# Local attention on Trainium2: the V product in four 64x64 quadrants, with the output projection in column halves

## The chip, the cores and the metric

The kernel runs on one core of one Trainium2 chip. The time is device time in microseconds (us) of one execution. Three runs of the kernel before took 3222.01, 3215.9 and 3220.32 us; the median is 3220.32 us.

## The reference, cut to what matters

The program is four layers of cross attention and feed-forward blocks on 128 sequences of 64 tokens with 128 features, all in fp32. The change touches only the last block, which holds two rounds (DEPTH = 2) of local attention, each followed by a gated MLP. With 64 tokens in a sequence and a window of 64, there is one window, so the attention is causal over the sequence itself:

```python
DIM, HEADS, DIM_HEAD, WINDOW = 128, 8, 64, 64      # INNER = 512
def _layer(x, wqkv, qs, ksc, wo, ...):             # x: 128 sequences x 64 tokens x 128
    h = shift_token(x)                             # half of the features come from the token before
    q, k, v = jnp.split(h @ wqkv, 3, axis=-1)      # each 512 wide: 8 heads of 64
    q = l2norm(q) * qs;  k = l2norm(k) * ksc
    q, k = rotary_xpos(q, k)
    sim = jnp.einsum('bhwid,bhwjd->bhwij', bq, bk) # bq is 8 * q
    attn = jax.nn.softmax(jnp.where(mask, -big, sim), axis=-1)
    out = jnp.einsum('bhwij,bhwjd->bhwid', attn, bv)
    x = x + o @ wo                                 # o: 512 wide, wo: 512x128
    ...                                            # gated MLP
```

## The kernel before, in words

The residual stream `x` stays in SBUF as 64 tiles of 128 tokens (two sequences of 64) by 128 features. `local_attention(l)` goes over these tiles in 16 groups of four (GT = 4). Every engine runs its own written-out order of steps, `body(g)`, once a group, in a hardware loop (`run_tiles`); semaphores tie the engines together, and `wait_tile(engine, signal, g, t)` waits until tile t has passed a step. The work is software pipelined: in the step for tile u, TensorE handles tiles u to u+3.

The order on TensorE for each u (a "tile turn" below) is:

- `scores(u+1)`, L1981 and L1989: a causal mask as four bf16 matmuls, then 16 matmuls of 64x64 stationary by 64 columns. Sequence b goes to the column half b (PSUM partitions 64b and on), the head parity j is the row half (SBUF partitions 64j and on) and the PSUM bank. So four (row half, column half) pairs follow one another.
- `project_qk(u+3)`, L1949 and L1950, and `project_v(u+3)`, L1960: V comes out with the parity of the head as the partition half.
- `weigh_values(u)`, L2014: the product V^T P^T, 16 matmuls of 64x64 by 64 columns into `ps_o`. Row half j writes column half j, for both sequences, so only two of the four pairs occur.
- in the first tile turn of a group, `transpose_window(g+1)`, L1941: four transposes for the next group.
- `turn_qk(u+2)`, L1970: eight 128x128 transposes of the normalised queries and keys.
- `project_o(u)`, L2022: four 128x128x128 matmuls that accumulate in `ps_pj`. It contracts over pairs of heads.
- `turn_probs(u+1)`, L2000: four transposes of the probabilities.

An fp32 matmul is two records in the trace, a transpose or a bf16 matmul is one.

The other engines: ScalarE squares q and k (L2059), takes the exponentials (L2082) and copies PSUM to SBUF (`copy_ot` L2092, `copy_v` L2072, `copy_qk` L2078, `copy_pt` L2087). VectorE does row maxima and the subtraction (L2187, L2190), row sums and the reciprocal (L2198, L2200), the rotary products (L2166 and L2173 twice), the squares' sums (L2178, L2181) and the residual (L2204). GpSimd adds the two rotary products (`unite`, L2130), refines the norms' inverse roots (L2136 to L2140), scales q and k with them (`normalise_qk`, L2143) and scales the probabilities (L2123). In the trace `kblk` is the room of the rotated q and k and of V, `big_flat` that of `qk_t`, `pl`, `pt` and `ot`.

Weights that are needed late are loaded by DMAs that GpSimd issues between its steps in the first cross attention (`late_loads`, issued at L743; 50 of them, five after each of ten groups).

Of the kernel before, what the change touches and what calls it, by code (L numbers as in the profile page):

```python
# [18 lines left out]
F32 = mybir.dt.float32  # L19
ACT = mybir.ActivationFunctionType  # L20
# [3 lines left out]
P = 128  # L24
S = 64
# [23 lines left out]
LHEADS, LD, LPAIRS = 8, 64, 4  # L49
INNER = LHEADS * LD  # L50
HALF = LD // 2
DEPTH = 2
# [35 lines left out]
def build_program(nc, w, x_in, ctx_t, mask_l2, mask_l3, out):  # L88

    with ExitStack() as ctx:  # L90
        def sb(name, shape, dt=F32):
            return ctx.enter_context(nc.sbuf_tensor(name, shape, dt))
# [3 lines left out]
        def signal(name, per=0, ahead=0):  # L96
            if name not in signals:
                assert per == 0 or name in GROUP_SIGNALS, name
                signals[name] = Signal(ctx.enter_context(nc.semaphore(name)))
            signals[name].opens(per, ahead)  # L100
            return signals[name]
# [75 lines left out]
        one_less_mu = {n: sb("one_less_mu_" + n, [P, 1]) for n in "rk"}  # L177
        w_qkv = [sb(f"w_qkv{l}", [P, 3 * INNER]) for l in range(DEPTH)]
        w_lo = [sb(f"w_lo{l}", [P, LPAIRS, P]) for l in range(DEPTH)]

        rot_base = sb("rot_base", [P, 4, LD])
        rot = [sb(f"rot{l}", [P, 4, LD]) for l in range(DEPTH)]
# [21 lines left out]
        ps_s = ctx.enter_context(nc.psum_tensor("ps_s", [P, 4, 512], F32))  # L204
        ps_scores = [ps_s[:, 2 * i:2 * i + 2, :] for i in range(2)]
        ps_pt = ctx.enter_context(nc.psum_tensor("ps_pt", [P, 2, 512], F32))
        ps_o = ctx.enter_context(nc.psum_tensor("ps_o", [P, 512], F32))
        ps_pj = ctx.enter_context(nc.psum_tensor("ps_pj", [P, 512], F32))


        carried = signal("carried", GT)
# [12 lines left out]
        late_loads = [(attn_w[n][:, :], w[n]) for n in attn_w if not n.startswith("L0")]  # L224
# [7 lines left out]
        late_loads += [(mu[n][:, :], w["mu_" + n]) for n in "rk"]  # L232
        late_loads += [(rot_base[:, :, :], w["rot"]), (rot_scale[:, :, :, :], w["rot_scale"])]
        for l in range(DEPTH):
            late_loads += [(w_qkv[l][:, :], w["wqkv"][l]), (w_lo[l][:, :, :], w["lo"][l]),
                           (w_up1[l][:, :], w["up1"][l]),
                           (b_up1[l][:, :], w["b_up1"][l]), (w_dn[l][:, :, :], w["dn"][l]),
                           (b_dn[l][:, :], w["b_dn"][l]), (ln_gb[l][:, :], w["ln"][l])]
# [171 lines left out]
        added = signal("added")  # L410
# [171 lines left out]
        def wait_past(eng, s, g, k):  # L582

            value = s.at(g, k)
            if not isinstance(value, int) or value > s.base:
                eng.wait_ge(s.sem, value)
# [1292 lines left out]
        def local_attention(l):  # L1879
# [25 lines left out]
            ot_copied = signal("ot_ready", GT)  # L1905
            y_ready = signal("y_ready", GT)

            bank_qk, bank_ts = ps_scores
            bank_v, bank_p = ps_pt[:, 0, :], ps_pt[:, 1, :]
            square = probs[0][:, :, :]  # L1910
            nrm, nlog, nroot, nstep = (small[n][:, 0, :] for n in "bcde")

# [6 lines left out]
            def wait_tile(eng, s, g, t, done=None):  # L1919

                each = s.per // GT
                wait_past(eng, s, g, each * t + (each if done is None else done))
# [4 lines left out]
            with nc.Block() as block:  # L1927
                @block.sync
                def _(sp):
                    move_window(sp, 1 if l == 0 else 0)  # L1930

                @block.tensor
                def _(pe):
# [69 lines left out]
                    def weigh_values(g, t):  # L2003
                        wait_tile(pe, pt_copied, g, t)
                        wait_tile(pe, v_copied, g, t)
                        wait_tile(pe, ot_copied, g, t - 1)
                        pe.sem_inc(pe_turn.sem, 1)
                        for r in range(LPAIRS):
                            for b in range(2):
                                tok = slice(r * P + b * S, r * P + (b + 1) * S)  # L2010
                                for j in range(2):
                                    rows = slice(j * S, (j + 1) * S)
                                    at = t % GT * INNER + b * 2 * P + r * LD
                                    last = pe.matmul(ps_o[rows, tok], v_rows[rows, at:at + LD], pt[rows, tok],  # L2014
                                                     start=True, stop=True)
                        last.then_inc(summed.sem, 1)

                    def project_o(g, t):
                        wait_tile(pe, ot_copied, g, t)
                        wait_tile(pe, added, g, t - 1)  # L2020
                        for r in range(LPAIRS):
                            last = pe.matmul(ps_pj[:, 0:P], ot[:, r * P:(r + 1) * P], w_lo[l][:, r, :],  # L2022
                                             start=r == 0, stop=r == LPAIRS - 1)
                        last.then_inc(y_ready.sem, 1)

                    def body(g):
# [20 lines left out]
                @block.scalar  # L2047
                def _(act):
                    act.preload_act_table_set(LN_EXP)

                    def copy_window(g):
                        act.wait_ge(xt_in_psum.sem, xt_in_psum.at(g, 1))
                        wait_tile(act, v_in_psum, g, -1)
                        act.activation(q_t[0][:, :], bank_p, ACT.Copy).then_inc(xt_ready.sem, 1)

                    def squares(g, t):
                        wait_tile(act, qk_in_psum, g, t)
                        wait_tile(act, norms, g, t - 1, 1)
                        act.activation(square.rearrange("p (i h) d -> p i (h d)", i=2), bank_qk, ACT.Square)\  # L2059
                           .then_inc(squared.sem, 1)  # L2060

                    def roots(g, t):
                        wait_tile(act, norms, g, t)
                        act.activation(nlog, nrm, ACT.Ln, scale=float(2 ** LOG_SCALE)).then_inc(l_root.sem, 1)
                        wait_tile(act, l_root, g, t, 1)
                        wait_tile(act, unit, g, t - 1)
                        act.activation(nroot, nlog, ACT.Exp, scale=-0.5).then_inc(l_root.sem, 1)

                    def copy_v(g, t):
                        wait_tile(act, v_in_psum, g, t)  # L2070
                        wait_tile(act, summed, g, t - GT)
                        act.activation(v_rows[:, t % GT * INNER:(t % GT + 1) * INNER], bank_v, ACT.Copy)\  # L2072
                           .then_inc(v_copied.sem, 1)

                    def copy_qk(g, t):
                        wait_tile(act, qk_turned, g, t)
                        wait_tile(act, scored, g, t - 1)
                        act.activation(qk_t, bank_ts, ACT.Copy).then_inc(qk_copied.sem, 1)  # L2078

                    def exponentials(g, t):  # L2080
                        wait_tile(act, shifted, g, t)
                        act.activation(pl[:, :], pl[:, :], ACT.Exp, scale=8.0).then_inc(exp_ready.sem, 1)  # L2082

                    def copy_pt(g, t):
                        wait_tile(act, turned, g, t)
                        wait_tile(act, summed, g, t - 1)
                        act.activation(pt[:, :], bank_p, ACT.Copy).then_inc(pt_copied.sem, 1)  # L2087

                    def copy_ot(g, t):
                        wait_tile(act, summed, g, t)  # L2090
                        wait_tile(act, y_ready, g, t - 1)
                        act.activation(ot[:, :], ps_o[:, :], ACT.Copy).then_inc(ot_copied.sem, 1)  # L2092

                    def body(g):
                        for u in range(GT):
                            now, next_ = has_tile(g, u), has_tile(g, u + 1)
                            if next_:
                                exponentials(g, u + 1)
                            if has_tile(g, u + 3):
                                squares(g, u + 3)  # L2100
                            if now:
                                copy_ot(g, u)
                            if has_tile(g, u + 3):
                                copy_v(g, u + 3)
                            if u == 0 and has(g + 1):
                                copy_window(g + 1)
                            if has_tile(g, u + 2):
                                copy_qk(g, u + 2)
                            if has_tile(g, u + 3):
                                roots(g, u + 3)  # L2110
                            if next_:
                                copy_pt(g, u + 1)

                    run_tiles(act, body)
# [252 lines left out]
        pl, pt, ot = (flat_big[:, i * INNER:(i + 1) * INNER] for i in (2, 3, 4))  # L2367
        v_rows = key_room[0][:, 0:GT * INNER]
# [121 lines left out]
```

## Time and profile before

| what | value |
| --- | --- |
| median of three runs | 3220.32 us |
| the profiled execution, its own time | 3222.59 us |
| its span | 3220.4 us |
| first local attention, about | 1937 to 2421 us |
| second local attention, about | 2575 to 3075 us |
| TensorE busy over the span | 2947.0 us, 92% |
| VectorE, ScalarE, GpSimd busy | 74%, 52%, 36% |

How to read it: all times in rows are us from the span's start, unless marked ns. PE is TensorE's matmuls, PEld its weight loads, DVE VectorE, ACT ScalarE, POOL GpSimd. A row of the timeline has the start, the length, the engine, the line in the kernel, the operation with its shapes, and the count of merged instructions; brackets hold the idle time before it and what ended that. The length of a matmul row includes the latency of its pipeline, so the next row starts before the last one has ended, and it is the distance from start to start that says what a step costs. Where the array was drained before a step, its first matmul is recorded from the start of its weight load.

### The profile page before, as it was taken

What the parts mean: (1) busy time and instruction counts of PE and PEld (TensorE: products, weight loads), DVE (VectorE), ACT (ScalarE), POOL (GpSimd) and SP (SyncE); (2) the same over time, 40 slices, a digit from 0 to 9 for tenths busy, and PEclk for the clock granted to TensorE, in tenths of its full rate; (3) what the DMA queues carried; (4) which work ended last, traced back from release to release, by engine and by line L of the source; (5) the groups of instructions that cost most, each with busy time, mean ns of one, the idle gap of its engine ahead of it and who ended that gap; (6) DMA issues with size and microseconds to landing.
All of it is one profiled execution on the core that took longest, in us unless ns stands there. A gap on an engine that the chain in (4) does not pass through costs nothing. (4 is left out here: it accounts for less than half of the span.)

```text
span 3220.4 us, 101185 instructions
## 1 busy us (share of the span) xinstructions
PE 2947.0 (92%) x37200; PEld 2073.1 (64%) x37200; DVE 2368.3 (74%) x5209; ACT 1660.7 (52%) x2660; POOL 1148.5 (36%) x1289
## 2 busy tenths in 40 slices
PE   5998669997999989998899969999998999999989
PEld 4776557775666657776667746666665566676655
DVE  6777767776777757776667767888876588888755
ACT  4675226664333335554366665666653356666522
POOL 4210221210000001110212108888862278888734
PEclk9999769998999999999999989999998999999989
DMA  3311001110000002111011110000001100000022
GB/s 94 92 39 24 7 10 28 28 31 18 0 0 0 0 21 42 40 40 24 8 32 43 45 33 8 10 10 10 6 4 33 26 9 10 10 10 6 4 81 76
DMA packets 190888, 81.28 MB, mean 25 GB/s; under 512 B 175953, under 2 KB 176528, under 8 KB 190240
## 3 DMA queue, kind: packets, MB, share of 16 engines
q1 hardware_dynamic: 187024, 69.14, 9.3%
q0 software_dynamic: 3728, 10.28, 1.0%
q8 instruction: 91, 1.49, 0.2%
q14 instruction: 45, 0.37, 0.0%
HBM read 37.55 MB, written 8.39 MB: 14 GB/s over the span
## 5 line engine op out<-in xcount | busy, mean ns | idle before, releaser
L593 POOL TENSOR_TENSOR x_norm<-x,mean_all 128x512 f32 (+1 forms) x80 | 83.3, 1042 | 1423.1 <-PE ps_pj L547 851.0
L751 DVE TENSOR_REDUCE row_max<-ps_s 128x16 f32<-128x1024 f32 x256 | 313.5, 1224 | 175.6 <-PE ps_s L990 172.1
L886 ACT ACTIVATE probs_t<-ps_pt 128x1024 f32<-128x1024 f32 x256 | 262.3, 1024 | 314.9 <-PE ps_pt L1001 314.9
L2130 POOL TENSOR_TENSOR kblk<-kblk 128x1024 f32<-128x1024 f32 x128 | 302.3, 2362 | 140.7 <-DVE kblk L2173 140.7
L757 DVE TENSOR_TENSOR probs<-ps_s,row_max 128x1024 f32<-128x1024 f32 x256 | 312.0, 1219 | 8.9
L1023 PEld LDWEIGHTS ps_o<-v,probs_t 128*64 128x64 f32 x8192 | 261.4, 138 | 40.6 <-issue 22.5
L1001 PE MATMUL ps_pt<-ident,probs 128*128 128x128 f32 x2048 | 283.1, 282 | 1.2 <-ACT probs L881 1.2
L1023 PE MATMUL ps_o<-v,probs_t 128*64 128x18 f32 x8192 | 283.7, 212 | 0.0
L881 ACT ACTIVATE probs<-probs 128x1024 f32<-128x1024 f32 x256 | 268.5, 1049 | 12.0 <-DVE probs L757 12.0
L2143 POOL TENSOR_TENSOR kblk<-kblk,small_d 128x1024 f32<-128x1024 f32 x128 | 243.6, 1903 | 19.0 <-POOL small_d L2140 17.7
L1001 PEld LDWEIGHTS ps_pt<-ident,probs 128*128 128x128 f32 x2048 | 222.3, 142 | 11.0 <-ACT probs L881 3.3
L1480 ACT ACTIVATE probs<-ps_s 128x512 f32<-128x512 f32 x128 | 76.7, 599 | 225.3 <-PE ps_pt L1427 225.1
L990 PE MATMUL ps_s<-kblk,q_t 32*64 32x256 f32 x4096 | 179.1, 406 | 7.4 <-DVE probs L757 5.4
L2166 DVE TENSOR_TENSOR kblk<-ps_s,rot 128x1024 f32<-128x1024 f32 x128 | 156.8, 1225 | 28.1 <-ACT probs L2059 27.3
L767 DVE RECIPROCAL rec<-ps_o 128x16 f32<-128x16 f32 x256 | 66.0, 258 | 138.6 <-PE ps_o L1031 95.3
L1436 PEld LDWEIGHTS ps_o<-w,probs 128*128 128x128 f32 x1024 | 133.0, 191 | 49.6 <-issue 25.5
L2014 PEld LDWEIGHTS ps_o<-big_flat,kblk 64*64 64x64 f32 x4096 | 131.1, 136 | 51.1 <-issue 51.1
L2173 DVE TENSOR_TENSOR kblk<-ps_s,rot 128x512 f32<-128x512 f32 x256 | 163.6, 681 | 0.0
L1970 PE MATMUL ps_s<-ident,kblk 128*128 128x128 f32 x1024 | 139.0, 279 | 23.1 <-POOL kblk L2143 21.2
L2198 DVE TENSOR_REDUCE row_max<-big_flat 128x8 f32<-128x512 f32 x128 | 87.8, 686 | 93.9 <-ACT big_flat L2082 93.9
L2178 DVE TENSOR_REDUCE floored<-probs 128x16 f32<-128x1024 f32 x128 | 154.7, 1208 | 0.0
L1949 PE MATMUL ps_s<-w_qkv,q_t 128*128 128x512 f32 x256 | 147.8, 660 | 5.9 <-DVE kblk L2173 4.4
(336 smaller groups left out, 6684.2 us busy)
## 6 DMA issues: line engine op xcount, KB each, us to landing
ci<-in_ctx_t SPq DMA_DIRECT2D x64, 256.0 KB, 3.0
kblk<-k_t SPq DMA_DIRECT2D x688, 16.0 KB
ci<-x SPq DMA_DIRECT2D x64, 128.0 KB
ci<-x SPq DMA_DIRECT2D x128, 63.0 KB
x<-in_x_in SPq DMA_DIRECT2D x4, 1024.0 KB, 8.3
mask<-in_mask_l SPq DMA_DIRECT2D x64, 64.0 KB, 2.5
out<-x SPq DMA_DIRECT2D x16, 256.0 KB, 2.0
out<-x POOLq DMA_DIRECT2D x16, 256.0 KB, 2.3
```

The costliest lines, as they stand in the source:

```text
L751: dve.tensor_reduce(by_group(row_max[u % 2][:, :]), scores_4, AX, ALU.max)\
L757: dve.tensor_tensor(probs[u % 2][:, :, :].rearrange("p (c h) k -> p c h k", c=RG), scores_4, by_group(row_max[u % 2][:, :]).unsqueeze(3).b ...
L881: act.activation(p, p, ACT.Exp, scale=scale).then_inc(exp_ready.sem, 1)
L886: act.activation(probs_t[:, :, :], ps_pt[:, :, :].rearrange("p a (r t) -> p (a r) t", t=P), ACT.Copy).then_inc(pt_ready.sem, 1)
L990: last = pe.matmul(score_banks[b * S:(b + 1) * S, c, :], q_t[par][rows, tok], kblk[par][rows, :, tok], start=plain, stop=True, skip_group_ ...
L1001: last = pe.transpose(ps_pt[:, r // 4, (r % 4) * P:(r % 4 + 1) * P], flat[:, r * P:(r + 1) * P], ident[:, :])
L1023: last = pe.matmul(accumulated[half, 2 * r:2 * r + 2, :], probs_t[:, r, half], v2[par][:, 2 * u + b, r, :, :], start=True, stop=True)
L2130: pool.tensor_tensor(a, a, b_, ALU.add).then_inc(rotated.sem, 1)
L2143: pool.tensor_tensor(a, a, nroot.unsqueeze(2).broadcast_to([P, 2 * LHEADS, LD]), ALU.mult)\
L2166: dve.tensor_tensor(a, by_half(bank_qk), table(0, 0, LD), ALU.mult).then_inc(products.sem, 1)
L2173: dve.tensor_tensor(b_[:, :, :, to:to + HALF], by_half(bank_qk)[:, :, :, of:of + HALF], table(1, to, HALF), ALU.mult).then_inc(products.se ...
L2178: dve.tensor_reduce(floored[:, :, 0], square, AX, ALU.add).then_inc(norms.sem, 1)
```

## The change

- In `weigh_values` the second sequence (b = 1) writes the opposite column half: row half j goes to column half 1 - j. The first sequence goes to one bank, the second to another: `ps_o` and `ps_pj` are now two halves of one tensor `ps_oj`, and `weighted` is columns 256 to 511 of both. It also waits for `added` of the tile before, since `ps_pj` is read by the residual.
- `copy_ot` reads both banks and stores the sequences one after the other.
- In `ot` the heads of the second sequence are thus swapped between the partition halves. `project_o` takes for it a second copy of the weights, `w_lo_turned`, with the halves swapped, and splits each of its four matmuls in two: one a sequence, 64 columns of stationary each, into the column half b of `ps_pj`.
- `w_lo_turned` is loaded by four more late loads, of 128 KB each.

```diff
+        w_lo_turned = [sb(f"w_lo_turned{l}", [P, LPAIRS, P]) for l in range(DEPTH)]
-        ps_o = ctx.enter_context(nc.psum_tensor("ps_o", [P, 512], F32))
-        ps_pj = ctx.enter_context(nc.psum_tensor("ps_pj", [P, 512], F32))
+        ps_oj = ctx.enter_context(nc.psum_tensor("ps_oj", [P, 2, 512], F32))
+        ps_o, ps_pj = (ps_oj[:, i, :] for i in range(2))
         for l in range(DEPTH):
+            late_loads += [(w_lo_turned[l][j * S:(j + 1) * S, :, :], w["lo"][l][(1 - j) * S:(2 - j) * S])
+                           for j in range(2)]
+            weighted = ps_oj[:, :, 2 * P:4 * P]
 # weigh_values
                         wait_tile(pe, ot_copied, g, t - 1)
+                        wait_tile(pe, added, g, t - 1)
...
-                                    last = pe.matmul(ps_o[rows, tok], v_rows[rows, at:at + LD], pt[rows, tok],
+                                    half = (1 - j if b else j) * S
+                                    last = pe.matmul(weighted[half:half + S, b, r * S:(r + 1) * S],
+                                                     v_rows[rows, at:at + LD], pt[rows, tok],
                                                      start=True, stop=True)
 # project_o
                         for r in range(LPAIRS):
-                            last = pe.matmul(ps_pj[:, 0:P], ot[:, r * P:(r + 1) * P], w_lo[l][:, r, :],
-                                             start=r == 0, stop=r == LPAIRS - 1)
+                            for b in range(2):
+                                at = (b * LPAIRS + r) * S
+                                weights = (w_lo, w_lo_turned)[b][l]
+                                last = pe.matmul(ps_pj[b * S:(b + 1) * S, 0:P], ot[:, at:at + S], weights[:, r, :],
+                                                 start=r == 0, stop=r == LPAIRS - 1)
 # copy_ot
-                        act.activation(ot[:, :], ps_o[:, :], ACT.Copy).then_inc(ot_copied.sem, 1)
+                        act.activation(ot.rearrange("p (b t) -> p b t", b=2), weighted, ACT.Copy)\
+                           .then_inc(ot_copied.sem, 1)
```

## Rows read from the trace of the kernel before

**Rows 1.** Busy time: us and instructions of each engine, granted clock, DMA share, GB/s.

```profile
2080.00:2160.00 80.00, 78.87 (x1108) 55.57 (x1107) 67.97 (x111) 50.67 (x92) 66.58 (x77) 1.00 0.03 7
```

**Rows 2.** Timeline: one tile turn, from one tile's maxima to the next's.

```profile
2235.09 0.69 DVE L2187 TENSOR_REDUCE row_max<-ps_s 128x8 f32<-128x512 f32 x1 [0.29 <-PE ps_s L1989]
...
2235.90 1.02 PE L1950 MATMUL ps_s<-w_qkv,q_t 128*128 128x512 f32 x2
...
2237.00 1.90 POOL L2143 TENSOR_TENSOR kblk<-kblk,small_d 128x1024 f32<-128x1024 f32 x1 [0.16 <-POOL small_d L2140]
2237.07 1.01 ACT L2059 ACTIVATE probs<-ps_s 128x1024 f32<-128x1024 f32 x1
...
2237.87 1.15 PE L2014 MATMUL ps_o<-big_flat,kblk 64*64 64x64 f32 x32
...
2238.11 1.22 DVE L2166 TENSOR_TENSOR kblk<-ps_s,rot 128x1024 f32<-128x1024 f32 x1
...
2239.03 1.09 PE L1970 MATMUL ps_s<-ident,kblk 128*128 128x128 f32 x8
...
2239.25 1.28 DVE L2173 TENSOR_TENSOR kblk<-ps_s,rot 128x512 f32<-128x512 f32 x2
...
2239.96 1.06 PE L2022 MATMUL ps_pj<-w_lo,big_flat 128*128 128x128 f32 x8
2240.16 1.03 ACT L2078 ACTIVATE big_flat<-ps_s 128x1024 f32<-128x1024 f32 x1
...
2240.71 2.37 POOL L2130 TENSOR_TENSOR kblk<-kblk 128x1024 f32<-128x1024 f32 x1 [0.80 <-DVE kblk L2173]
...
2240.85 0.60 PE L2000 MATMUL ps_pt<-ident,big_flat 128*128 128x128 f32 x4
...
2241.38 0.30 PE L1981 MATMUL ps_s<-mask_causal,ident 64*64 64x256 bf16 x4
...
2241.51 0.63 PE L1989 MATMUL ps_s<-big_flat 64*64 64x64 f32 x32
...
2241.92 0.29 DVE L2204 TENSOR_TENSOR x<-x,ps_pj 128x128 f32 x1
...
2242.32 0.69 DVE L2187 TENSOR_REDUCE row_max<-ps_s 128x8 f32<-128x512 f32 x1
```

**Rows 3.** Timeline: further maxima and turns of the tiles around it.

```profile
2212.96 0.69 DVE L2187 TENSOR_REDUCE row_max<-ps_s 128x8 f32<-128x512 f32 x1
...
2220.47 0.69 DVE L2187 TENSOR_REDUCE row_max<-ps_s 128x8 f32<-128x512 f32 x1 [0.21 <-PE ps_s L1989]
...
2224.47 1.09 PE L1970 MATMUL ps_s<-ident,kblk 128*128 128x128 f32 x8
...
2227.67 0.69 DVE L2187 TENSOR_REDUCE row_max<-ps_s 128x8 f32<-128x512 f32 x1
...
2231.89 1.09 PE L1970 MATMUL ps_s<-ident,kblk 128*128 128x128 f32 x8 [0.30 <-POOL kblk L2143]
```

**Rows 4.** Timeline: where a group begins, with the window's transposes.

```profile
2244.42 1.90 POOL L2143 TENSOR_TENSOR kblk<-kblk,small_d 128x1024 f32<-128x1024 f32 x1 [0.16 <-POOL small_d L2140]
...
2246.58 0.38 PE L1970 MATMUL ps_s<-ident,kblk 128*128 128x128 f32 x2
...
2249.75 0.69 DVE L2187 TENSOR_REDUCE row_max<-ps_s 128x8 f32<-128x512 f32 x1
```

**Rows 5.** Timeline of the channel mix: transposes, matmuls in column halves, full matmuls.

```profile
1526.88 0.60 PE L547 MATMUL ps_pj<-ident,x_norm 128*128 128x128 f32 x4
1527.41 0.45 PE L1654 MATMUL ps_s<-probs_t,ci 128*64 128x128 f32 x4
...
1528.99 0.44 PE L1655 MATMUL ps_s<-probs_t,ci 128*64 128x128 f32 x4
1529.36 1.13 PE L1645 MATMUL ps_s<-ci,probs_t 128*128 128x512 f32 x2
```

**Rows 6.** Groups of instructions on POOL while the late weights load.

```profile
L743 POOL DMA_DIRECT2D w_lo<-in_lo x2 | 1.1, 543 | 0.0
```

## The prediction

> **What bounds the kernel now.** I read the busy time by engine first, for the two local attentions, since the change touches nothing else but a few loads. TensorE is busy 78.87 of 80 us there at the full granted clock, VectorE 67.97 and GpSimd 66.58 [rows 1]. That looks like a TensorE bound, and it would make every nanosecond saved there count. So I read a tile turn in order of time next, and asked of each engine what it waited for.
>
> TensorE's turn_qk starts at 2239.03, and GpSimd's normalise_qk, which it needs, ends at 2237.00 + 1.90 = 2238.90 [rows 2]. The matmuls before it, L2014, are recorded 1.15 us long from 2237.87 and so end at 2239.02 with their pipeline's latency; TensorE just fills the time until GpSimd is done. The same delay of about 0.13 us behind GpSimd holds in most turns. So the length of a turn is set by a loop through all engines, and TensorE's high busy share is a coincidence of two limits. I follow this loop from the row maxima of one tile ("max", L2187):
>
> - max at 2235.09; rotary product L2166 at 2238.11 (it waits on VectorE for the sums and on ScalarE for the squares, L2059, which end at 2238.08: both arrive together); the second product L2173 ends at 2239.25 + 1.28 = 2240.53; GpSimd's unite starts at 2240.71 [rows 2], and normalise_qk of that tile ends at 2244.42 + 1.90 = 2246.32 [rows 4]. From max to there 11.23 us, and turn_qk can start 0.13 later: 11.36 us.
> - turn_qk at 2239.03, project_o at 2239.96 (0.93), turn_probs at 2240.85 (0.89), the mask at 2241.38 (0.53), the next max at 2242.32 (0.94; VectorE's residual ended at 2242.21) [rows 2]. From turn to max 3.29 us, 2.35 of it until the mask; in other turns 3.20.
>
> Together they span two turns, so two such loops run side by side, each closed once a group of four:
>
> - B: 2212.96 -> turn 2224.47 (11.51) -> 2227.67 (3.20) -> turn 2239.03 (11.36) -> 2242.32 (3.29): 29.36 us [rows 2, 3].
> - A: 2220.47 -> turn 2231.89 (11.42) -> 2235.09 (3.20) -> turn 2246.58 (11.49) -> 2249.75 (3.17): 29.28 us [rows 2 to 4].
>
> In A the turn at 2246.58 is 0.26 behind GpSimd's end at 2246.32 instead of 0.13 [rows 4]: only there, once a group, is TensorE itself late, by 0.13 us, because the window's transposes stand before it. In B, 0.09 of the 3.29 is VectorE's: its residual ended just before. So a group takes 29.32 us, and of that a faster TensorE ahead of turn_qk can remove about 0.1.
>
> **The V product.** 32 records in two (row, column) pairs take 1.15 us (L2014); the scores' 32 records of the same shape, in four pairs, 0.63 us (L1989) [rows 2]. The new order also visits four pairs in turn, one bank for each sequence, and within a column half the two row halves always write different banks, as in the scores. So it saves 0.52 us of TensorE per tile, 67 us over 128 tiles. It lies wholly before turn_qk, which waits for GpSimd. Worth on the path: the 0.13 of loop A. If the four pairs should not overlap, the saving is nought and loop A keeps its 0.13, which loop B covers; so the bounds here are 0 and 0.13 us a group, and B decides.
>
> The added wait for `added` of the tile before costs nothing: that residual (L2204) is issued before the max, and the V product starts 2.78 us after the max (2237.87 against 2235.09) [rows 2]. Behind the wait stand the V product, turn_qk and project_o, which would all be late if that cover were gone. copy_ot reads two banks with the same 512 columns and now starts about 0.5 us earlier; project_o, which needs it, is ordered behind turn_qk. The residual (L2204) comes after L2178 in VectorE's order, so an end of project_o that is some tenths later is hidden.
>
> **The output projection.** It has the same arithmetic but another tiling of the array: 64 columns of stationary, two column halves. This form stands in the channel mix: 32 records of 128*64 by 128 columns from 1527.41 to 1529.36, 1.95 us [rows 5]. Three costs, all between turn_qk and the mask:
>
> 1. Into the halves. Four transposes followed by such matmuls take 0.53 from start to start (1526.88 to 1527.41) [rows 5], as do four transposes before the scores' 64x64 form (2240.85 to 2241.38). Eight transposes followed by project_o in the same full form take 0.93 including a first weight load of about 0.05 [rows 2], so 0.11 each, 0.44 for four: a change of form costs 0.09 before the next weight load starts. turn_qk to project_o: 0.93 + 0.09 = 1.02.
> 2. project_o itself: of the 1.95 us, 0.05 are the first load and 0.09 the drain at the end, 1.81 the 16 pairs, 0.113 a pair. Eight pairs: 0.90 + 0.14 = 1.04, against 0.89 now. At 0.109 a pair, as a lone 128-column stream takes here, it would be 1.01.
> 3. turn_probs then starts with a load that nothing hides: 0.53 + 0.05 = 0.58.
>
> Sum 1.02 + 1.04 + 0.58 = 2.64, against 2.35: about +0.29 us, which I round to +0.30 because the tiles' accumulation in two groups is not in the rows. The Trainium skill has a rule for this: in "TensorEngine Tiling (Array Packing)", Key Properties, a change of tiling mode drains TensorE, and the change adds two to a turn; by that rule the trace agrees, with 0.09 us and an exposed load each time. Bounds: below, the copy of q and k (L2078) ends at 2241.19, so if the mask waits for it and not for TensorE, at most 0.19 - 0.13 = 0.06 of the +0.30 is hidden: +0.24. Above, if the halves did not overlap at all, 16 x 0.11 = 1.76 + 0.14 = 1.90: +1.15 in all. I take 0.30, since rows 5 show this very form.
>
> Loop A then takes 11.42 + 11.36 + 2 x (3.19 + 0.30) = 29.76, loop B 11.51 + 11.36 + 2 x (3.20 + 0.30) = 29.87, VectorE's 0.09 hidden by the longer turn. B sets the pace: 29.87 - 29.32 = +0.55 us a group. Of 32 groups some 30 run in the steady state: +16.5 us. VectorE alone needs per turn 2242.21 - 2235.09 = 7.12, and TensorE after the change less than now, so neither ends later than 29.87 / 4 = 7.47.
>
> **The rest.** At the end of each layer the last two tiles pass the V product with nothing beside it: 4 x 0.52 = -2 us. Four more loads of 128 KB go out on GpSimd's queue, at 0.54 us each to issue [rows 6], six after a group instead of five, while GpSimd is idle most of the time; they also share the DMA engines with the keys' placement. 0 to +1 us, taken as +0.5. The clock: TensorE stays busy 90% and more of each turn, so I expect the full 1.00 of rows 1.
>
> Sum: +16.5 - 2 + 0.5 = +15 us. On the profiled execution's 3222.59 us (span 3220.4) that is 3237.6; on the median of 3220.32 us, 3235.
>
> **The rivals.**
>
> - *TensorE is the bound after all.* For it: 98.6% busy. Then each tile saves 0.52 - 0.30 = 0.22 us, 128 tiles 28 us: 3192 us. Against it: turn_qk follows GpSimd by a fixed 0.13 us in three turns of four, and GpSimd's start is tied to VectorE. It decides only if the 11.36 us of the other engines shrink when TensorE is less busy. The Trainium skill has, in "Perfetto Trace Analysis", Identifying the Most-Contended Engine, the rule to optimise the engine with the highest occupancy first; read that way this rival would be the forecast, though the page itself warns against TensorE's busy share. Chance 0.08.
> - *The changes of form are cheaper than in the other stage,* 0.05 or less in all. Then only the small gains are left: loop B at 29.27, -0.05 x 30, and the ends' -2: 3217 us, no measurable change. For it: in the rows the change also goes with another wait. Against it: both kinds, into 64x64 and into 128x64, show the same 0.53. Chance 0.12.
> - *The column halves don't overlap* here because both accumulate in one bank: 29.32 becomes 11.51 + 11.36 + 2 x 4.35 = 31.57, +72 us less 2: 3290 us. Rows 5 show two accumulating groups in halves of one bank overlapping. Chance 0.04.
>
> **How the numbers follow.** The forecast, slower by loop B, has 0.76; its own range is 3228 (bound +0.24, fewer steady groups) to 3243 (+0.35). The range for 8 in 10 adds most of the middle between it and the second rival: 3222 to 3243. Less than 0.2%, 6.4 us, can't be told from no change. Faster: first rival and a part of the second, 0.10. Same: most of the second and the lowest end of the forecast, 0.15. Slower: 0.75.
>
> **What would show it.** L2014 about 0.63 us long per tile, and a wait of TensorE for GpSimd before L1970 of 0.3 to 0.6 us in nearly every turn (the saving turned into idle time). turn_qk to mask 2.6 to 2.7 us instead of 2.35; the lines of project_o split into 16 records with pairs 0.11 apart; max to turn unchanged at 11.4 to 11.5; turns 7.45 to 7.5 us apart. Wrong, if turn to mask stays at 2.35, if max to turn shortens, if project_o's records stand 0.11 apart singly, or if the granted clock falls below 1.00 in these stages.

## The result and the profile after

The changed kernel takes 3235.17 us in the median (3229.13 to 3238.82, five runs) against 3219.74 (3215.9 to 3222.01, five runs): ratio 1.0047, 95% interval 1.0033 to 1.0062. It is slower by 15 us, half a per cent; the interval stands for 11 to 20 us. The profiled execution took 3236.37 us, its span is 3234.3.

The busy time of the changed kernel in the same 80 us of the first local attention as [rows 1], with the same columns:

```profile
2080.00:2160.00 80.00, 75.81 (x1187) 49.02 (x1186) 66.42 (x109) 49.93 (x88) 65.60 (x76) 1.00 0.03 7
```

TensorE is less busy (75.81 against 78.87), the granted clock is still 1.00, and VectorE and GpSimd are less busy too: everything turns more slowly. The timeline of one tile turn of the changed kernel, as in [rows 2] (L2198 is the max, L1974 turn_qk, L2020 the V product, L2032 the projection, L2004 turn_probs, L1985 the mask, L2154 normalise_qk, L2088 copy_qk):

```profile
2059.88 0.69 DVE L2198 TENSOR_REDUCE row_max<-ps_s 128x8 f32<-128x512 f32 x1 [0.24 <-PE ps_s L1993]
...
2061.84 1.90 POOL L2154 TENSOR_TENSOR kblk<-kblk,small_d 128x1024 f32<-128x1024 f32 x1 [0.16 <-POOL small_d L2151]
...
2062.66 0.69 PE L2020 MATMUL ps_oj<-big_flat,kblk 64*64 64x64 f32 x32
...
2063.87 1.09 PE L1974 MATMUL ps_s<-ident,kblk 128*128 128x128 f32 x8 [0.51 <-POOL kblk L2154]
...
2064.89 0.32 PE L2032 MATMUL ps_oj<-w_lo,big_flat 128*64 128x128 f32 x1
2064.90 0.32 PE L2032 MATMUL ps_oj<-w_lo_turned,big_flat 128*64 128x128 f32 x1
...
2065.00 1.02 ACT L2088 ACTIVATE big_flat<-ps_s 128x1024 f32<-128x1024 f32 x1 [0.48 <-PE ps_s L1974]
2065.05 0.27 PE L2032 MATMUL ps_oj<-w_lo,big_flat 128*64 128x128 f32 x1
2065.06 0.27 PE L2032 MATMUL ps_oj<-w_lo_turned,big_flat 128*64 128x128 f32 x1
2065.16 0.27 PE L2032 MATMUL ps_oj<-w_lo,big_flat 128*64 128x128 f32 x1
...
2065.91 0.65 PE L2004 MATMUL ps_pt<-ident,big_flat 128*128 128x128 f32 x4
2066.50 0.30 PE L1985 MATMUL ps_s<-mask_causal,ident 64*64 64x256 bf16 x4
...
2067.34 0.69 DVE L2198 TENSOR_REDUCE row_max<-ps_s 128x8 f32<-128x512 f32 x1 [0.34 <-PE ps_s L1993]
```

The V product is 0.69 us long instead of 1.15. What it saved stands as idle time before turn_qk: 0.51 us, waiting for normalise_qk, which ended at 2063.74. From turn_qk to the mask it is now 2066.50 - 2063.87 = 2.63 us, against 2.35 in [rows 2]. VectorE waits 0.34 us for the scores before the max.

The next rows give the loops, with turn_qk of the tile turn that has the window's transposes at 2071.24:

```profile
2071.24 1.09 PE L1974 MATMUL ps_s<-ident,kblk 128*128 128x128 f32 x8
...
2074.74 0.69 DVE L2198 TENSOR_REDUCE row_max<-ps_s 128x8 f32<-128x512 f32 x1
...
2078.84 1.09 PE L1974 MATMUL ps_s<-ident,kblk 128*128 128x128 f32 x8 [0.65 <-POOL kblk L2154]
...
2082.32 0.69 DVE L2198 TENSOR_REDUCE row_max<-ps_s 128x8 f32<-128x512 f32 x1 [0.38 <-PE ps_s L1993]
...
2086.16 1.09 PE L1974 MATMUL ps_s<-ident,kblk 128*128 128x128 f32 x8 [0.37 <-POOL kblk L2154]
...
2089.63 0.69 DVE L2198 TENSOR_REDUCE row_max<-ps_s 128x8 f32<-128x512 f32 x1 [0.19 <-PE ps_s L1993]
...
2093.67 1.09 PE L1974 MATMUL ps_s<-ident,kblk 128*128 128x128 f32 x8 [0.56 <-POOL kblk L2154]
...
2097.14 0.69 DVE L2198 TENSOR_REDUCE row_max<-ps_s 128x8 f32<-128x512 f32 x1 [0.38 <-PE ps_s L1993]
```

Loop A: 2059.88 -> 2071.24 (11.36) -> 2074.74 (3.50) -> 2086.16 (11.42) -> 2089.63 (3.47): 29.75 us, against 29.28 in [rows 2 to 4]. Loop B: 2067.34 -> 2078.84 (11.50) -> 2082.32 (3.48) -> 2093.67 (11.35) -> 2097.14 (3.47): 29.80, against 29.36 in [rows 2, 3]. The parts from max to turn are those of before, and A has lost the 0.13 us by which TensorE was late. The whole increase is in the parts from turn to max.

How long each stage is can be read from its first and last max, 63 turns apart. The instructions of that line in the two stages, kernel before and kernel after (minimum, median and maximum in ns, then first and last start in us):

```profile
L2187 DVE TENSOR_REDUCE row_max<-ps_s x64: 681/692/693, 1941.7 to 2404.8; 128x8 f32<-128x512 f32 x64
L2187 DVE TENSOR_REDUCE row_max<-ps_s x64: 681/692/693, 2588.0 to 3053.2; 128x8 f32<-128x512 f32 x64
```

```profile
L2198 DVE TENSOR_REDUCE row_max<-ps_s x64: 679/692/693, 1939.7 to 2412.6; 128x8 f32<-128x512 f32 x64
L2198 DVE TENSOR_REDUCE row_max<-ps_s x64: 690/692/692, 2595.2 to 3068.0; 128x8 f32<-128x512 f32 x64
```

463.1 + 465.2 = 928.3 us before, 472.9 + 472.8 = 945.7 after: +17.4 us in the two stages, against +13.9 in the span. The same view from the 9th to the 57th max, 12 groups of four turns, leaves out how a stage fills and empties (before, then after):

```profile
L2187 DVE TENSOR_REDUCE row_max<-ps_s x49: 691/692/693, 2000.6 to 2352.4; 128x8 f32<-128x512 f32 x49
L2187 DVE TENSOR_REDUCE row_max<-ps_s x49: 684/692/693, 2646.1 to 3000.6; 128x8 f32<-128x512 f32 x49
```

```profile
L2198 DVE TENSOR_REDUCE row_max<-ps_s x49: 690/692/693, 2000.5 to 2357.9; 128x8 f32<-128x512 f32 x49
L2198 DVE TENSOR_REDUCE row_max<-ps_s x49: 690/692/692, 2654.6 to 3013.4; 128x8 f32<-128x512 f32 x49
```

A group takes 29.32 us in the first stage and 29.54 in the second before, 29.78 and 29.90 after: +0.47 and +0.36. The 24 groups between these rows hold 9.9 of the 17.4 us; the 15 turns at the start and end of each stage hold the other 7.5, where that rate would give 3.1. The granted clock in them was lower than in the middle, and lower after than before in three of four: 0.96 against 0.98 at the start of the first stage, 0.94 against 0.97 at the end of both; it was 1.00 in both kernels over all the groups in the middle. Whether the clock makes that difference was not tried.

The first max of the first stage already varies between 1936.9 and 1947.9 us among the profiled runs of this study, in work that no edit but the late loads touches, so differences of a few us in the whole are not told apart by one profile. For every experiment I therefore give the sum of the two stages' lengths, and the length of a group of four turns in the middle of each.

### The profile page after: what moved, and what is told of

Read it like the earlier page. It is cut to its first block and busy times, and to the rows that moved or that the text cites. A ratio compares the mean times of both kernels' runs of the same rounds, so it can differ in the third digit from the quotient of the medians.

```text
span 3234.3 us, 103317 instructions
## 1 busy us (share of the span) xinstructions
PE 2925.3 (90%) x38192; PEld 2002.2 (62%) x38224; DVE 2366.8 (73%) x5209; ACT 1662.2 (51%) x2660; POOL 1149.9 (36%) x1293
## 5 line engine op out<-in xcount | busy, mean ns | idle before, releaser
L1026 PEld LDWEIGHTS ps_oj<-v,probs_t 128*64 128x64 f32 x8192 | 261.8, 138 | 40.9 <-issue 22.9
L1026 PE MATMUL ps_oj<-v,probs_t 128*64 128x18 f32 x8192 | 284.1, 212 | 0.0
L2154 POOL TENSOR_TENSOR kblk<-kblk,small_d 128x1024 f32<-128x1024 f32 x128 | 243.6, 1903 | 20.4 <-POOL small_d L2151 19.1
L1974 PE MATMUL ps_s<-ident,kblk 128*128 128x128 f32 x1024 | 141.5, 282 | 57.4 <-POOL kblk L2154 57.0
L770 DVE RECIPROCAL rec<-ps_oj 128x16 f32<-128x16 f32 x256 | 65.9, 257 | 137.1 <-PE ps_oj L1034 92.7
L1439 PEld LDWEIGHTS ps_oj<-w,probs 128*128 128x128 f32 x1024 | 133.0, 191 | 49.5 <-issue 25.5
L2088 ACT ACTIVATE big_flat<-ps_s 128x1024 f32<-128x1024 f32 x128 | 131.4, 1027 | 59.2 <-PE ps_s L1974 58.9
L1974 PEld LDWEIGHTS ps_s<-ident,kblk 128*128 128x128 f32 x1024 | 112.0, 143 | 75.7 <-issue 59.3
```

The lines of the kernel that those rows point to most:

```text
L1026: last = pe.matmul(accumulated[half, 2 * r:2 * r + 2, :], probs_t[:, r, half], v2[par][:, 2 * u + b, r, :, :], start=True, stop=True)
L1974: last = pe.transpose(bank_ts[:, i, r * P:(r + 1) * P], rotated_qk[t % 2][:, i * INNER + r * P:i * INNER + (r + 1) * P], ident[:, :])
L2154: pool.tensor_tensor(a, a, nroot.unsqueeze(2).broadcast_to([P, 2 * LHEADS, LD]), ALU.mult)\
```

## The experiments

Theory: two loops through all engines set the pace; what TensorE saves ahead of turn_qk is hidden by GpSimd, and what it loses between turn_qk and the mask is not. Rivals: TensorE's total is the bound; the slowdown comes from elsewhere (banks, the added wait, the split matmuls).

| kernel | median us | before, same set of runs | ratio, 95% interval | both stages, us | a group, us |
| --- | --- | --- | --- | --- | --- |
| before | 3219.74 | | | 928.3 | 29.32, 29.54 |
| after | 3235.17 | 3219.74 | 1.0047 (1.0033 to 1.0062) | 945.7 | 29.78, 29.90 |
| e1 quadrants only | 3219.01 | 3216.74 | 1.0005 (0.9996 to 1.0014) | 924.8 | 29.24, 29.41 |
| e2 halves only | 3238.46 | 3216.74 | 1.0067 (1.0053 to 1.0081) | 948.1 | 30.05, 30.06 |
| e3 after, no refinement | 3177.91 | 3216.74 | 0.9879 (0.9864 to 0.9894) | 891.9 | 28.22, 28.39 |
| e4 after, turn_probs first | 3237.06 | 3216.74 | 1.0050 (1.0037 to 1.0064) | 941.2 | 29.64, 29.82 |
| e5 before, half projection | 3212.66 | 3218.42 | 0.9988 (0.9977 to 0.9998) | 920.7 | 29.20, 29.33 |
| e6 before, a step to ScalarE | 3201.46 | 3218.42 | 0.9949 (0.9934 to 0.9963) | 910.9 | 28.90, 29.04 |
| e7 after, a step to ScalarE | 3217.11 | 3218.42 | 1.0000 (0.9990 to 1.0009) | 923.8 | 29.22, 29.33 |
| e8 before, no refinement | 3193.73 | 3218.42 | 0.9927 (0.9912 to 0.9942) | 905.2 | 28.74, 28.90 |

The changed kernel, e1 to e4 and e5 to e8 were run as three sets, each beside its own runs of the kernel before; where two kernels of different sets are compared, the ratios are the fairer measure.

**e1: the V product alone.** The changed kernel, with the projection and `copy_ot` so, and without `w_lo_turned` and its loads:

```diff
-                            for b in range(2):
-                                at = (b * LPAIRS + r) * S
-                                weights = (w_lo, w_lo_turned)[b][l]
-                                last = pe.matmul(ps_pj[b * S:(b + 1) * S, 0:P], ot[:, at:at + S], weights[:, r, :],
-                                                 start=r == 0, stop=r == LPAIRS - 1)
+                            last = pe.matmul(ps_pj[:, 0:P], ot[:, r * P:(r + 1) * P], w_lo[l][:, r, :],
+                                             start=r == 0, stop=r == LPAIRS - 1)
-                        act.activation(ot.rearrange("p (b t) -> p b t", b=2), weighted, ACT.Copy)\
+                        act.activation(ot.rearrange("p (r b t) -> p b r t", b=2, t=S),
+                                       weighted.rearrange("p b (r t) -> p b r t", t=S), ACT.Copy)\
```

> The V product in four quadrants and two banks as in the changed kernel, but the output projection in the full 128x128 form with the old weights, and without w_lo_turned. For the second sequence the heads thus meet the wrong rows of w_lo, so only the time counts. Loop theory (two loops through all engines set the pace, TensorE's saving before turn_qk is hidden): turn_qk to mask stays 2.35 us, loop B of a group is 11.51 + 11.36 + 2 x 3.20 = 29.27 against 29.32 before, ends -2: 3215 to 3218 us, no measurable change from before; TensorE's wait before turn_qk grows to about 0.5 us a turn. Rival (TensorE is the bound): 0.52 us less for each of 128 tiles, -67 us, about 3153 us.

No measurable change in the whole, as the theory had it (3219.01 is 1 us above its 3215 to 3218); the rival's 3153 us is out of the question. In the middle of the stages a group is 0.08 and 0.13 us shorter, about the small gain of loop A (0.05 a group in the sum). Its timeline:

```profile
2037.12 1.90 POOL L2149 TENSOR_TENSOR kblk<-kblk,small_d 128x1024 f32<-128x1024 f32 x1 [0.16 <-POOL small_d L2146]
...
2037.84 0.69 PE L2017 MATMUL ps_oj<-big_flat,kblk 64*64 64x64 f32 x32
...
2039.15 1.09 PE L1971 MATMUL ps_s<-ident,kblk 128*128 128x128 f32 x8 [0.62 <-POOL kblk L2149]
...
2041.50 0.30 PE L1982 MATMUL ps_s<-mask_causal,ident 64*64 64x256 bf16 x4
```

The V product is as short as in the changed kernel, its saving stands as idle time in front of turn_qk (0.62 us), and the mask follows 2.35 us after. Two banks, the added wait and the copy from two banks are in this kernel, so they cost nothing that can be measured.

**e2: the column halves alone.** The kernel before, with

```diff
-                            last = pe.matmul(ps_pj[:, 0:P], ot[:, r * P:(r + 1) * P], w_lo[l][:, r, :],
-                                             start=r == 0, stop=r == LPAIRS - 1)
+                            for b in range(2):
+                                at = r * P + b * S
+                                last = pe.matmul(ps_pj[b * S:(b + 1) * S, 0:P], ot[:, at:at + S], w_lo[l][:, r, :],
+                                                 start=r == 0, stop=r == LPAIRS - 1)
```

> The kernel before with only the output projection split into column halves (the full result, same weights for both halves); the V product in two pairs as before. Loop theory: turn_qk to mask 2.63 us instead of 2.35, and with the V product still long, the turn_qk of the tile turn with the window's transposes is held by TensorE at 4.34 us after the maxima while GpSimd is done for it at 3.90: loop A is 11.42 + 11.36 + 0.44 + 2 x 3.47 = 30.16 against 29.32, +0.84 a group, 30 groups: +25 us, 3245 us. Rival (TensorE is the bound): +0.28 for each of 128 tiles, +36 us, 3256 us. Rival (the change of tiling mode costs nothing, the slowdown comes from elsewhere, as the two banks or the added wait): 3220 us.

+21.7 us; the stages are 19.8 us longer. So the halves make the whole slowdown, with neither the four more loads nor the second bank. That they cost more here than in the changed kernel is seen in the groups (30.05 against 29.78 and 30.06 against 29.90 us), while the intervals of the two medians overlap. It is the part that the V product still plays, in the turn with the window's transposes:

```profile
2038.63 0.69 DVE L2189 TENSOR_REDUCE row_max<-ps_s 128x8 f32<-128x512 f32 x1 [0.21 <-PE ps_s L1989]
...
2040.61 1.90 POOL L2145 TENSOR_TENSOR kblk<-kblk,small_d 128x1024 f32<-128x1024 f32 x1 [0.16 <-POOL small_d L2142]
...
2041.41 1.15 PE L2014 MATMUL ps_o<-big_flat,kblk 64*64 64x64 f32 x32
...
2042.98 1.04 PE L1970 MATMUL ps_s<-ident,kblk 128*128 128x128 f32 x8
```

GpSimd was done at 2042.51, TensorE started turn_qk at 2042.98, 0.47 behind it instead of 0.13. The expected 25 us were 3 too many, and the sum shows why: it added the whole 0.44 to a part from max to turn of 11.36 that already holds the usual 0.13. With 0.44 - 0.13 = 0.31 loop A is 30.03 us, +0.71 a group or +21 us, and the groups measured 30.05 and 30.06.

**e5: what else holds the mask.** The kernel before with `for r in range(2)` and `stop=r == 1` in project_o.

> The kernel before with only two of the four matmuls of project_o (pairs of heads 2 and 3 are left out of the output projection). It asks what else holds the mask behind turn_qk. Loop theory: the mask also needs copy_qk on ScalarE, which ends 2.16 us after turn_qk and reaches TensorE 0.13 to 0.19 later, so turn to mask falls from 2.35 to 2.30 at best: -0.1 a group, 3214 to 3218 us. Rival (TensorE's own work between turn_qk and the mask sets its length alone): 0.45 us less per turn, 0.9 a group, -27 us, 3190 us. Rival (TensorE's total is the bound): -0.45 x 128 = -57 us, 3160 us.

-5.8 us, ratio 0.9988 (0.9977 to 0.9998): a small step, not the 27 or 57 us of the rivals. It is larger than the 3 us expected: 3212.66 lies below 3214 to 3218, a group is 0.12 and 0.21 us shorter instead of 0.1. The first is twice the 0.06 of the rows below; what makes the second larger was not followed up. The timeline shows why 0.45 us of TensorE's work between turn_qk and the mask are worth 0.06 a turn:

```profile
2027.11 1.09 PE L1970 MATMUL ps_s<-ident,kblk 128*128 128x128 f32 x8 [0.17 <-POOL kblk L2143]
...
2028.03 0.61 PE L2022 MATMUL ps_pj<-w_lo,big_flat 128*128 128x128 f32 x4
...
2028.23 1.02 ACT L2078 ACTIVATE big_flat<-ps_s 128x1024 f32<-128x1024 f32 x1 [0.16 <-PE ps_s L1970]
...
2028.48 0.60 PE L2000 MATMUL ps_pt<-ident,big_flat 128*128 128x128 f32 x4
...
2029.40 0.30 PE L1981 MATMUL ps_s<-mask_causal,ident 64*64 64x256 bf16 x4 [0.32 <-ACT big_flat L2078]
```

2.29 us from turn_qk to the mask, which now waits for copy_qk. In the kernel before the two arrive almost together, so TensorE had nothing to gain there beyond this 0.06, and everything that it is later counts. So TensorE and not copy_qk set the 2.35, and nothing of the halves' +0.28 was hidden, which the prediction's lower bound had left open.

**e4: one change of form less.** The changed kernel, with turn_probs ahead of project_o where u is not 0:

```diff
-                            if now:
+                            if now and u == 0:
                                 project_o(g, u)
                             if next_:
                                 turn_probs(g, u + 1)
+                            if now and u != 0:
+                                project_o(g, u)
```

> The changed kernel with turn_probs ahead of project_o in three of four tile turns (not in the one with the window's transposes, where turn_probs would wait for the window's copy). Then the full-form transposes are neighbours, and the projection's halves stand directly before the 64x64 scores, so one change of tiling mode a turn is gone. Mode-change theory: turn_qk to mask 2.63 - 0.14 = 2.49 us in these turns, loop B 29.55, loop A 29.58 against 29.83: -0.25 x 30 = -8 us against the changed kernel, 3227 us. Rival (the +0.28 is the split matmuls themselves, not the change of mode): no change, 3235 us.

The stages are 4.5 us shorter than in the changed kernel and the groups 0.14 and 0.08 us, where 0.25 was expected. The median is not shorter (3237.06, from runs of 3229.39 to 3238.66, and the intervals overlap): in the whole this is inconclusive.

```profile
2067.18 1.05 POOL L2136 TENSOR_TENSOR big_flat<-big_flat,row_max 128x512 f32<-128x512 f32 x1
...
2067.36 1.09 PE L1974 MATMUL ps_s<-ident,kblk 128*128 128x128 f32 x8 [0.42 <-POOL kblk L2156]
...
2068.29 0.66 PE L2004 MATMUL ps_pt<-ident,big_flat 128*128 128x128 f32 x4
...
2068.87 0.32 PE L2032 MATMUL ps_oj<-w_lo,big_flat 128*64 128x128 f32 x1
...
2069.90 0.30 PE L1985 MATMUL ps_s<-mask_causal,ident 64*64 64x256 bf16 x4
```

2.54 us from turn_qk to the mask: 0.09 less than 2.63, not 0.14. That fits the drain's 0.09 alone (the time in which the array empties before it takes another form); the 0.05 of the exposed load, a weight load that no matmul covers, are still there: turn_probs needs GpSimd's scaled probabilities (L2136), done at 2068.23, and can't load its weights behind turn_qk's matmuls. That this wait keeps the load exposed is read from these rows and was not tried by itself.

**e3 and e8: the loop shortened, after and before.** Of GpSimd's four small operations three are left out (the refinement of the inverse norms), in both kernels alike:

```diff
                         step(pool.tensor_tensor(nstep, nroot, nroot, ALU.mult))
-                        step(pool.tensor_tensor(nstep, nstep, nrm, ALU.mult))
-                        pool.sem_inc(pool_turn.sem, 1)
-                        step(pool.tensor_scalar(nstep, nstep, -0.5 * 2 ** LOG_SCALE, 1.5, ALU.mult, ALU.add))
-                        step(pool.tensor_tensor(nroot, nroot, nstep, ALU.mult))
```

> The changed kernel without three of GpSimd's four small operations that refine the inverse norms before normalise_qk (the refinement is left out). Loop theory: max to turn_qk shrinks by about 1.0 us, loop B from 29.83 to 27.8 a group, and VectorE's own 28.9 becomes the bound: -0.9 x 30 = -28 us against the changed kernel, about 3207 us, and TensorE waits less before turn_qk. Rival (TensorE or ScalarE is the bound): no change from 3235 us, since no work of theirs is touched.

> The kernel before without three of the four small operations (the refinement of the inverse norms is left out), to compare with the changed kernel without them (3178 us). With the loop shortened by 2 us a group the loop theory makes TensorE the bound in the kernel before: 3 turns of 7.05 and one of 7.51, 28.66 a group, -21 us, 3196 us, while the changed kernel has 28.2. So here the change should be worth -15 to -18 us instead of +15: its effect turns with what bounds the turn. Rival (the change costs +0.28 us a turn wherever it stands): the kernel before without the refinement is faster than 3178 us, about 3163.

Three GpSimd operations of 0.2 us each with the waits between them, nothing of TensorE's, take 57 us off the changed kernel (54 by the ratios) and 25 off the kernel before. The order of the two turns over: with the long loop the change costs 15 us, with the short one it gains 16 (3177.91 against 3193.73; 15 by the ratios, whose intervals, up to 0.9894 and from 0.9912, do not touch). The busy times in the stretch of [rows 1] say why, e3 first:

```profile
2080.00:2160.00 80.00, 79.58 (x1254) 52.54 (x1254) 69.77 (x115) 52.83 (x95) 61.75 (x46) 1.00 0.04 10
```

```profile
2080.00:2160.00 80.00, 80.00 (x1115) 56.73 (x1115) 69.07 (x112) 51.44 (x93) 61.06 (x46) 1.00 0.04 10
```

Without the refinement the kernel before has TensorE busy all the time, and turn_qk no longer follows GpSimd:

```profile
2102.81 1.90 POOL L2139 TENSOR_TENSOR kblk<-kblk,small_d 128x1024 f32<-128x1024 f32 x1
...
2105.46 1.09 PE L1970 MATMUL ps_s<-ident,kblk 128*128 128x128 f32 x8
```

GpSimd was done at 2104.71, and TensorE comes 0.75 us later instead of 0.13. So there TensorE is the bound, and there the V product's saving less the halves' price counts. By the rows it is 0.46 - 0.28 = 0.18 us a turn, 23 us in all; 13 to 16 came, so the changed kernel then meets another limit; which one was not tried. In e3 turn_qk starts 0.13 behind GpSimd again in three turns of four and 0.58 in the one with the window's transposes. e3 came out faster than my 3207: I had taken VectorE's 7.12 us a turn as its own minimum, as the prediction did, but its shortest turns in e3 are 6.92 and its groups 28.22 and 28.39 us, under four times 7.12. That figure was elapsed time up to the end of the residual's record, with 0.69 us of waiting for the exponentials in it, and not work; in e3 the next max starts 0.20 us behind the residual's start, before its record of 0.29 has ended.

**e6 and e7: the same lever with the refinement kept.** One of the four operations goes to ScalarE as a third small activation:

```diff
                         act.activation(nroot, nlog, ACT.Exp, scale=-0.5).then_inc(l_root.sem, 1)
+                        wait_tile(act, l_root, g, t, 2)
+                        act.activation(nstep, nroot, ACT.Square, scale=(0.5 * 2 ** LOG_SCALE) ** 0.5)\
+                           .then_inc(l_root.sem, 1)
...
-                        step(pool.tensor_tensor(nstep, nroot, nroot, ALU.mult))
                         step(pool.tensor_tensor(nstep, nstep, nrm, ALU.mult))
-                        step(pool.tensor_scalar(nstep, nstep, -0.5 * 2 ** LOG_SCALE, 1.5, ALU.mult, ALU.add))
+                        step(pool.tensor_scalar(nstep, nstep, -1.0, 1.5, ALU.mult, ALU.add))
```

> The kernel before with one of GpSimd's four small operations ahead of normalise_qk moved to ScalarE (the square of the root, a third small activation after the two roots). Loop theory: max to turn_qk 0.32 us shorter; loop B 29.36 - 0.64 = 28.7 a group, but loop A then meets TensorE in the tile turn with the window's transposes (turn_qk not before 4.34 us after the maxima, GpSimd ready at 3.83): 29.05. -0.27 x 30 = -8 us, 3209 us. Rival (TensorE is the bound): no change. Rival (ScalarE's added 0.22 us is on the path): slower, +0.22 x 128 = +28 us.

> The changed kernel with the same step moved from GpSimd to ScalarE. Loop theory: loop B 29.83 - 0.64 = 29.19, loop A 29.72 - 0.64 + 0.17 = 29.25: -0.58 x 30 = -17 us against the changed kernel, 3218 us, still behind the kernel before with the same edit.

e7 met its number (3217.11 against 3218; 18 us less than the changed kernel, 15 by the ratios). e6 gained 17 us where I had expected 8. The sum made the same mistake as e2's: it charged 0.51 us once a group for the window's transposes on top of a part that already holds 0.13. With 0.38 loop A is 28.92 us, and the groups measured 28.90 and 29.04, 0.42 and 0.50 less than before. The 28 us that ScalarE's added work would cost on the path did not come. At 3201.46 us, e6, which leaves nothing out, is the fastest full version of this study: 0.5% under the kernel before and, by the two ratios, 1% under the changed one.

## Why the prediction was right

It gave 3235 us in 3222 to 3243; measured 3235.17. The mechanism is shown; that the number is met to within 1 us is in part luck, as the last step says. By its steps:

- *Loops and not TensorE's total set the pace.* Shown: e1 takes 0.46 us of TensorE's time out of each tile turn and gains nothing that the median shows, e3 and e8 take three small operations of GpSimd's out and gain 57 and 25 us.
- *V product.* Expected 0.63 us long, worth at most the 0.13 of loop A. It is 0.69 long, and e1's ratio is 1.0005; its groups are 0.08 and 0.13 us shorter. The idle time before turn_qk was expected at 0.3 to 0.6 in nearly every turn; the rows above have 0.37 to 0.65 in three turns of four, and none in the one with the window's transposes, which fill it.
- *Added wait, two banks, copy_ot.* Expected nought; e1 has all three and shows nought.
- *Projection in halves.* 1.02 + 1.04 + 0.58 was the sum; the rows of the changed kernel have 1.02 (2063.87 to 2064.89), 1.02 and 0.59: 2.63 us. Rounded up to 2.65, it was 0.02 too much. The records come in pairs 0.11 apart, one in each half. That the +0.28 is the changes of form and not the splitting: the middle term is 1.02 with a drain and a load in it, so the own time of its eight pairs, 0.88, is no more than the full form's 0.89, and e4, with one change of form less, is 0.09 us shorter there.
- *Loops after.* Expected 29.76 (A) and 29.87 (B), measured 29.75 and 29.80 in the group shown, 29.78 and 29.90 as the mean of a group in the two stages. The two are too close to say that B sets the pace. Before, the second stage had 29.54 a group, which the 29.32 of the rows from the first stage did not show, so the step is +0.47 and +0.36 instead of +0.55: for 30 groups 12 us and not 16.5.
- *Max to turn_qk unchanged* at 11.35 to 11.50: so it is.
- *VectorE's own 7.12 us a turn* was no minimum, as e3 shows; at 7.45 us a turn nothing hung on it.
- *The rest.* -2 for the ends and +0.5 for the loads can't be told from the scatter of the other stages. From first to last max, which leaves out the V products that the -2 is about, the stages grew by 17.4 us where +16.5 was expected: 12 by the groups' rate for 30 of them, the rest by the slower turns at the start and end of each stage, which the prediction did not have. Outside them the profiled execution was 3.5 us shorter. Errors of 4 and 5 us thus cancelled.

The rivals: the one by TensorE's occupancy (3192 us) is refuted for this kernel by e1; e8 shows the condition under which it holds: once the other engines' part of the loop is shorter, TensorE is the bound. The one with cheap changes of form fell with e2, the one with halves that don't overlap with the pairs in the timeline.

## What to carry to other kernels

An engine that is 98% busy need not be the bound: look whether its next step starts a fixed time after another engine's end, and close the loop over as many turns as the pipeline has in flight. A saving then counts only in the segment that waits for nobody, and only as far as the next arrival there (0.45 us less work was worth 0.06 in e5); a new cost in that segment counts in full, however small it is beside the saving; splitting matmuls into another tiling between full-form neighbours cost a drain and an exposed weight load on each side here. When a change of this kind fails, the place to work is the other part of the loop, and work there may turn the sign of the first change. And where two parts are added, see that a delay held in one is not charged again in the other.

## What the runs showed of the hardware

- A change of TensorE's tiling form cost about 0.09 us before the next weight load, and that load (0.05 us) is exposed: the two changes added to a turn cost 0.28 us together (2.35 to 2.63), and one change less gave back 0.09 (e4, 2.54). The matmuls themselves were not slower in halves: eight pairs in 0.88 us against eight records in 0.89.
- Four 64x64 pairs overlap also when each row half alternates between two banks: 32 records in 0.69 us against 1.15 in two pairs, little more than the 0.63 of the scores, where each row half keeps its bank.
- A VectorE record can outlast the start of the next one on the same engine: in e3 the max starts 0.20 us behind the residual, whose record is 0.29 us long.
